# Attention's value product: the last key tile as doubled half tiles, the odd key apart, keys dealt to groups by 400

## The chip, the cores and the metric

The kernel runs on one core of a Trainium2 chip. The metric is the device time of one execution in microseconds (us); lower is better. A core has five engines with queues of their own: TensorE (PE in the profile; its weight loads are PEld), VectorE (DVE), ScalarE (ACT), GpSimd (POOL) and SyncE (SP), which here only issues the DMA transfers. They meet through semaphores.

## The reference, cut to what matters

Cross attention of 64 queries for each of 32 batches over 1601 context rows, 16 heads, then a recurrent mixing layer and a two-layer feed-forward, each with a residual. The change touches the attention alone:

```python
q = query @ w_q
k, v = jnp.split(context @ w_kv, 2, axis=-1)
scores = jnp.einsum('bhqd,bhkd->bhqk', q, k) * SCALE
attn = jax.nn.softmax(scores, axis=-1)
out = jnp.einsum('bhqk,bhkd->bhqd', attn, v)
```

The kernel multiplies the queries by the key weights first (`write_queries`), so that the scores are a product with the raw context (192 columns), and it multiplies the softmax with the raw context too; the value weights come in a later stage (`attention_output`). A product in full fp32 accuracy is made of fp32r products: a tensor x is split in x_hi (rounded) and x_lo = x - x_hi.

## The kernel before

`attend_batches` runs 32 batches of 8 steps, 256 steps in all; a step is 128 query rows (of the 16 x 64) against all 1601 keys. The loop holds two batches (16 steps) a pass. In step s the engines do this, each in its own order:

- TensorE: 20 matmuls of the scores of step s, in four chunks of 288, 512, 512 and 290 keys, then the product of step s-4 (`product`, LAG = 4): 13 key tiles of 128 keys, each with two matmuls, `pt_hi` against 384 columns (the context's high and low part side by side, `nat`), and `pt_lo` against 192 columns (the high part). The product of one step starts as its first low half (`pt_lo_done`) is there, and needs the second from the seventh tile on.
- VectorE: row maxima of the left and of the right half of the scores (L714, L716), their combination (L719), the output of the product of step s-5 (`out`, L695 and L701), then, when both exponentials are done, a transpose of the whole probability row in 32x32 blocks (L725, 1664 columns with 63 of padding) into `turned`, the sum of the row (L726) and its reciprocal (L728).
- ScalarE: `high` (L614) rounds the landed, transposed probabilities of step s-4 to `pt_hi` in two halves of 6 and 7 tiles, `half_out` (L605) scales half of the accumulator, a piece of the next batch is rounded in some steps, then come the two exponentials of step s (L646). There is one `pt_hi`, so `high` waits for the product before to end (`acc_ready`), and for the transfers of its pair of steps (`moved`).
- GpSimd: `low` (L550), the two halves of `pt_lo`, and one piece of the next batch in most steps.
- SyncE issues every transfer of the stage, in program order. `move(m)` (L485) carries two steps' blocks from `turned` to `landed` in 16 transfers, since a block of keys has to change its partitions. `load_raw(n + 1)` (L452) fetches the next batch's context rows. A batch n of the queue is: `load_ct_a`, `move(4n-1)`, `load_qk`, `store`, `load_qk`, `move(4n)`, `load_raw`, `load_ct_b` (L464, L465), `move(4n+1)`, `load_ct_b`, `store`, `move(4n+2)`, `load_ct_a`. `move(m)` waits until the transposes of steps 2m and 2m+1 are done.

Keys sit in four groups of 32 partitions. Before, group g takes 416 keys in a row (13 tiles of 32), and the last group gets the 353 that are left and zeros. So the context rows of a batch come in five transfers:

```python
    for g in reversed(range(GROUPS)):
        tiles, at = (TILES if g < GROUPS - 1 else whole), g * TILES * ROWS
        rows = src[at:at + tiles * ROWS, :].rearrange("(t x) c -> x t c", x=ROWS)
        yield raw[g * ROWS:(g + 1) * ROWS, 0:tiles, :], rows
```

Of the kernel before, what the change touches and what calls it, by code (L numbers as in the profile page):

```python
# [37 lines left out]

GROUPS, ROWS = 4, 32
TILES = -(-NKV // P)  # L40
PADDED = GROUPS * TILES * ROWS
HALVES = [(0, 802), (802, NKV + NKV % 2)]
# [48 lines left out]
def write_queries(nc, x, w_q, wkT, qk_dram, ctx_in, ctxT_in, shared, turned):  # L91
# [7 lines left out]
    with ExitStack() as ctx:  # L99
# [30 lines left out]
        padded, raw_free, first_in = sem("padded"), sem("raw_free"), sem("first_in")  # L130
        first_a, first_q, first_b = first_views(turned)
# [7 lines left out]
        def _(sp):  # L139
# [21 lines left out]
            sp.wait_ge(raw_free, 1)  # L161
# [11 lines left out]
            sp.wait_ge(first_in, 16 * (3 + GROUPS + 1 + 3))  # L173

        @block.gpsimd
        def _(pool):
            identity(nc, pool, ident, ident_done)
            nc.gpsimd.memset(turned[:, :, NKV:NKV + 1], 0.0).then_inc(padded, 1)

            pool.wait_ge(wq_hi_done, 1)  # L180
            nc.gpsimd.tensor_tensor(wq_lo[:, :, :], wq[:, :, :], bits(wq_hi[:, :, :]), ALU.subtract).then_inc(wq_lo_done, 1)
            pool.wait_ge(wk_hi_done, 1)
            nc.gpsimd.tensor_tensor(wks_lo[:, :, :], wks[:, :, :], bits(wks_hi[:, :, :]), ALU.subtract).then_inc(wk_lo_done, 1)
            pool.wait_ge(wk_lo_done, 1)
            pool.wait_ge(tp_ready, NT)
            nc.gpsimd.memset(raw[(GROUPS - 1) * ROWS:P, :, :], 0.0).then_inc(raw_free, 1)
# [184 lines left out]
def attend_batches(nc, ctx_in, ctxT_in, qk_dram, o_dram, shared, turned):  # L371
# [15 lines left out]
    CW = NKV + NKV % 2  # L387
# [7 lines left out]
    with ExitStack() as ctx:  # L395
# [14 lines left out]
        part, o_q = sb("part", [P, DC]), sb("o_q", [P, DC])  # L410
        o_t = shared[:, KT * DC:KT * DC + DC * SB].rearrange("p (k s x) -> p k s x", s=SB, x=R)
# [20 lines left out]
        acc_ready, part_done, acc_read, o_done = sem("acc_ready"), sem("part_done"), sem("acc_read"), sem("o_done")  # L432
# [3 lines left out]
        first_a, first_q, first_b = first_views(turned)  # L436
# [12 lines left out]
        def _(sp):  # L449
# [46 lines left out]
            def body(r, first, last):  # L496
                for u in range(SPB):
# [32 lines left out]
            sp.wait_ge(padded, 2)  # L530
# [10 lines left out]
        def _(pool):  # L541

            nc.gpsimd.memset(stage[:, 1, NKV - CHALF[1][0]:CW - CHALF[1][0]], 0.0).then_inc(padded, 1)
            nc.gpsimd.memset(prob[:, NKV:PW], 0.0).then_inc(padded, 1)
# [52 lines left out]
        def _(act):  # L597
            def half_out(p, ring, par, fresh):

                act.wait_ge(acc_ready, p + 1)  # L600
                act.wait_ge(rinv_done, p + 1)
                if not fresh:

                    act.wait_ge(acc_read, p)
                nc.scalar.activation(part[:, :], acc[par][:, DC:2 * DC], ACT.Copy, scale=rinv[:, ring:ring + 1]).then_inc(part_done, 1)  # L605

            def high(p, count, slot, fresh):

                act.wait_ge(moved[slot // 2], count)
                if not fresh:  # L610

                    act.wait_ge(acc_ready, p)
                for t0, t1 in THALF:
                    nc.scalar.activation(pt_hi[:, t0:t1, :, :], by_tile(slot, t0, t1), ACT.Copy).then_inc(pt_hi_done, 1)  # L614
# [15 lines left out]
            def prepare_nat(n, h, par, fresh):  # L630

                t0, t1 = THALF[h]
                act.wait_ge(raw_in, n * 80)
                if not fresh:

                    act.wait_ge(acc_ready, n * SB - SB)
                nc.scalar.activation(nat[par][:, t0:t1, 0:DC], raw[:, t0:t1, :], ACT.Copy).then_inc(nat_hi_done, 1)

            def step(r, j, first):
                s, par = r * SPP + j, j % 2  # L640
                act.wait_ge(max_done, s + 1)
                if not (first and j == 0):

                    act.wait_ge(turned_done, s)
                for h, (lo, hi, done) in enumerate(((0, MID, exp_left), (MID, NKV, exp_done))):
                    nc.scalar.activation(prob[:, lo:hi], scores[:, S0 + lo:S0 + hi], ACT.Exp, bias=negmax[:, par:par + 1],  # L646
                                         accum_out=rowsum[:, par, h:h + 1]).then_inc(done, 1)

            def drain(r, j, first):
                if not (first and j < LAG + 1):  # L650
                    half_out(r * SPP + (j - LAG - 1), (j - LAG - 1) % SB, (j - LAG - 1) % 2, first and j == LAG + 1)
# [20 lines left out]
            for h, (lo, hi) in enumerate(CHALF):  # L672
# [15 lines left out]
        def _(dve):  # L688
            def out(p, ring, par, fresh_half, first):

                dve.wait_ge(part_done, p + 1)
# [19 lines left out]
            def step(r, j, first):  # L711
# [16 lines left out]
                nc.vector.reciprocal(rinv[:, j % SB:j % SB + 1], rowtot[:, par:par + 1]).then_inc(rinv_done, 1)  # L728

# [4 lines left out]

            lower = slice(DCB, P)
# [20 lines left out]
        def _(pe):  # L756
# [21 lines left out]
            def product(r, j, first):  # L778
# [5 lines left out]
                for h, (t0, t1) in enumerate(THALF):  # L784
# [803 lines left out]
```

## Time and profile before

| | |
|---|---|
| median of 3 runs | 2571.8 us (2565.84 to 2573.11) |
| the profiled execution: time | 2574.86 us |
| its span, first to last instruction | 2573.1 us |
| attention's steady stretch (200 to 2067 us) | 1867 us, TensorE busy 1862 us of it |
| granted TensorE clock, whole span | 0.958 |

The profile is of one execution. Busy time counts an engine's instructions; matmuls are pipelined, so a matmul's duration is longer than the distance from its start to the start of the next. "Landing" is the time from the issue of a transfer until its semaphore is raised. SPq is SP's queue: there an instruction's duration is the time in which it is being issued. What is rated is the difference to the runs' median.

### The profile page before, as it was taken

The numbers are of one execution on the slowest core, as the hardware profiler recorded it, in microseconds if no ns is written. First come the engines' busy times: TensorE is split into PE (matmuls) and PEld (weight loads), VectorE is DVE, ScalarE is ACT, GpSimd is POOL, SyncE is SP. The second block draws the span as 40 slices with busy tenths as digits, with TensorE's granted clock in tenths as the row PEclk, the third lists the DMA queues.
The fourth block names the chain that finished last, engine by engine and source line by source line (L and its number), as shares of the span: only waits on it lengthen the run. The fifth ranks groups of instructions, "written<-read, shape, count | busy, mean of one in ns | idle before, by whom it ended". The sixth has DMA issues, their size and how long they took to land. (4 is left out here: it accounts for less than half of the span.)

```text
span 2573.1 us, 43052 instructions
## 1 busy us (share of the span) xinstructions
PE 2355.1 (92%) x13872; PEld 2145.3 (83%) x13872; DVE 1710.9 (66%) x2666; ACT 1516.0 (59%) x2459; POOL 1700.7 (66%) x873
## 2 busy tenths in 40 slices
PE   4969999999999999999999999999999947855777
PEld 3649999999999999999999999999999945744666
DVE  7766666666666666666666666666666626768762
ACT  4646666666666666666666666666666525543342
POOL 2007788888888888888888888888888632023452
PEclk9989999999999999999999999999999968986888
DMA  5957878888788888888777788878888549910000
GB/s 158 259 155 190 193 193 198 194 192 193 194 192 195 199 194 195 197 198 197 192 193 195 192 193 200 196 192 199 196 198 195 131 102 219 187 50 0 9 9 17
DMA packets 387378, 434.18 MB, mean 169 GB/s; under 512 B 45652, under 2 KB 362232, under 8 KB 387320
## 3 DMA queue, kind: packets, MB, share of 16 engines
q1 hardware_dynamic: 387320, 433.45, 69.2%
q8 instruction: 32, 0.52, 0.1%
q14 instruction: 26, 0.21, 0.0%
HBM read 162.73 MB, written 52.43 MB: 84 GB/s over the span
## 5 line engine op out<-in xcount | busy, mean ns | idle before, releaser
L550 POOL TENSOR_TENSOR p_pt_lo<-p_landed,p_pt_hi 128x768 fp32r<-128x768 f32 (+1 forms) x512 | 1005.1, 1985 | 359.9 <-ACT p_pt_hi L614 359.9
L789 PE MATMUL p_acc<-p_nat,p_pt_hi 128*128 128x384 f32 x3328 | 978.5, 362 | 14.1 <-POOL p_pt_lo L550 13.8
L791 PE MATMUL p_acc<-p_nat,p_pt_lo 128*128 128x192 f32 x3328 | 845.7, 254 | 0.0
L646 ACT ACTIVATE p_prob<-p_scores,p_negmax 128x800 f32<-128x800 f32 (+1 forms) x512 | 471.2, 926 | 515.7 <-DVE p_negmax L719 515.7
L773 PE MATMUL p_scores<-p_ct_hi,p_q_hi 128*128 128x512 f32 (+2 forms) x2048 | 710.2, 350 | 24.2 <-DVE p_ct_hi L746 13.8
L773 PE MATMUL p_scores<-p_ct_hi,p_q_lo 128*128 128x512 f32 (+2 forms) x2048 | 705.1, 348 | 0.0
L725 DVE STREAM_TRANSPOSE turned<-p_prob 128x1664 f32<-128x1664 f32 x256 | 489.5, 1912 | 317.0 <-ACT p_prob L646 317.0
L789 PEld LDWEIGHTS p_acc<-p_nat,p_pt_hi 128*128 128x128 f32 x3328 | 630.7, 190 | 16.5 <-issue 13.7
L791 PEld LDWEIGHTS p_acc<-p_nat,p_pt_lo 128*128 128x128 f32 x3328 | 640.8, 193 | 0.0
L614 ACT ACTIVATE p_pt_hi<-p_landed 128x768 fp32r<-128x768 f32 (+1 forms) x512 | 432.3, 892 | 159.2 <-PE p_acc L791 152.5
L773 PEld LDWEIGHTS p_scores<-p_ct_hi,p_q_hi 128*128 128x128 f32 x2048 | 388.8, 190 | 71.9 <-issue 14.3
L773 PEld LDWEIGHTS p_scores<-p_ct_hi,p_q_lo 128*128 128x128 f32 x2048 | 390.7, 191 | 44.7
L716 DVE TENSOR_REDUCE p_halfmax<-p_scores 128x1 f32<-128x801 f32 x256 | 254.1, 993 | 212.7 <-PE p_scores L773 212.7
L773 PE MATMUL p_scores<-p_ct_lo,p_q_hi 128*128 128x512 f32 (+2 forms) x1024 | 354.2, 346 | 0.0
L714 DVE TENSOR_REDUCE p_halfmax<-p_scores 128x1 f32<-128x800 f32 x256 | 253.7, 991 | 59.5 <-PE p_scores L773 52.3
L773 PEld LDWEIGHTS p_scores<-p_ct_lo,p_q_hi 128*128 128x128 f32 x1024 | 194.3, 190 | 22.3
L577 POOL TENSOR_TENSOR p_nat<-shared,p_nat 128x1152 fp32r<-128x1152 f32 (+1 forms) x62 | 178.5, 2879 | 0.0
L562 POOL TENSOR_TENSOR p_q_lo<-p_stage,p_q_hi 128x1024 fp32r<-128x1024 f32 x62 | 148.5, 2395 | 15.2 <-ACT p_q_hi L624 15.2
L695 DVE SCALAR_TENSOR_TENSOR p_o_q<-p_acc,p_rinv,p_part 128x192 f32<-128x192 f32 x256 | 107.0, 418 | 35.3 <-ACT p_part L605 34.4
L605 ACT ACTIVATE p_part<-p_acc,p_rinv 128x192 f32<-128x192 f32 x256 | 103.0, 402 | 31.4 <-PE p_acc L791 31.4
L558 POOL TENSOR_TENSOR p_ct_lo<-p_stage,p_ct_hi 128x802 fp32r<-128x802 f32 (+1 forms) x62 | 109.5, 1767 | 14.2 <-ACT p_ct_hi L621 14.2
L569 POOL TENSOR_TENSOR p_ct_hi<-p_stage,p_ct_hi 64x802 fp32r<-64x802 f32 (+1 forms) x62 | 109.0, 1757 | 5.6 <-POOL p_pt_lo L550 0.5
(190 smaller groups left out, 2652.9 us busy)
## 6 DMA issues: line engine op xcount, KB each, us to landing
p_landed<-turned SPq DMA_DIRECT2D x2048, 104.0 KB, 2.2
shared<-in_ctx SPq DMA_DIRECT2D x96, 312.0 KB
o_scratch<-shared SPq DMA_DIRECT2D x256, 96.0 KB, 2.6
qk_scratch<-p_out_a SPq DMA_DIRECT2D x16, 1024.0 KB, 4.6
p_oa<-o_scratch SPq DMA_DIRECT2D x32, 512.0 KB, 6.0
p_stage<-qk_scratch SPq DMA_DIRECT2D x31, 512.0 KB, 3.9
p_stage<-qk_scratch SPq DMA_DIRECT2D x62, 256.0 KB, 4.2
p_stage<-in_ctxT SPq DMA_DIRECT2D x31, 401.0 KB, 3.2
```

What stands on the lines that cost most here:

```text
L550: nc.gpsimd.tensor_tensor(pt_lo[:, t0:t1, :, :], by_tile(slot, t0, t1), bits(pt_hi[:, t0:t1, :, :]), ALU.subtract).then_inc(pt_lo_done, 1)
L558: nc.gpsimd.tensor_tensor(ct_lo[1 - par][:, lo:hi], stage[:, u, 0:hi - lo], bits(ct_hi[1 - par][:, 0, lo:hi]), ALU.subtract).then_inc(ct_a ...
L562: nc.gpsimd.tensor_tensor(stepped(q_lo[1 - par][:, u - 3, :]), by_step(stage[:, u - 3, :]), bits(stepped(q_hi[1 - par][:, u - 3, :])), ALU ...
L577: nc.gpsimd.tensor_tensor(x[:, t0:t1, DC:2 * DC], raw[:, t0:t1, :], bits(x[:, t0:t1, 0:DC]), ALU.subtract).then_inc(nat_done, 1)
L614: nc.scalar.activation(pt_hi[:, t0:t1, :, :], by_tile(slot, t0, t1), ACT.Copy).then_inc(pt_hi_done, 1)
L646: nc.scalar.activation(prob[:, lo:hi], scores[:, S0 + lo:S0 + hi], ACT.Exp, bias=negmax[:, par:par + 1], accum_out=rowsum[:, par, h:h + 1] ...
L714: nc.vector.tensor_reduce(halfmax[:, par, 0:1], scores[:, S0:S0 + MID], AX.X, ALU.max, negate=True).then_inc(halfmax_done, 1)
L716: nc.vector.tensor_reduce(halfmax[:, par, 1:2], scores[:, S0 + MID:S0 + NKV], AX.X, ALU.max, negate=True).then_inc(halfmax_done, 1)
L725: nc.vector.transpose(turned[:, j % 4, :], prob[:, :]).then_inc(turned_done, 1)
L773: last = nc.tensor.matmul(scores[:, S0 + lo:S0 + hi], w, x, start=m == 0, stop=m == len(terms) - 1)
L789: nc.tensor.matmul(acc[k % 2][:, 0:2 * DC], pt_hi[:, t, :, :].rearrange("p i x -> p (i x)"), x[:, t, :], start=t == 0, stop=False, skip_gr ...
L791: last = nc.tensor.matmul(acc[k % 2][:, 0:DC], pt_lo[:, t, :, :].rearrange("p i x -> p (i x)"), x[:, t, 0:DC], start=False, stop=t == KT - ...
```

## The change

Group g now takes 400 keys in a row, 12 whole tiles of 32 and 16 more. The 1600 keys so make 12 whole tiles of 128, and a thirteenth that holds 64 keys twice: in each group's 32 partitions 16 keys, and the same 16 again. `pt_hi` of this tile is `landed` times a column `second` that is 0 in the first sixteen and 1 in the second sixteen partitions of each group; `pt_lo` = landed - `pt_hi` is then the whole probability in the first and the low part in the second. One matmul of `pt_lo` against 384 columns does the tile, where two stood. Key 1601, the odd one, is left out of the product: VectorE keeps its probability and multiplies it by the reciprocal of the row sum, ScalarE scales the key's context row with it (a row held on all partitions, one more transfer a batch), and VectorE adds both halves of the accumulator to this in two instructions.

```diff
 def raw_pieces(raw, ctx_in, n):
     src = ctx_in[bass.ds(n, 1), :, :].rearrange("a k c -> (a k) c")
-    whole = (NKV - (GROUPS - 1) * TILES * ROWS) // ROWS
     for g in reversed(range(GROUPS)):
-        tiles, at = (TILES if g < GROUPS - 1 else whole), g * TILES * ROWS
-        rows = src[at:at + tiles * ROWS, :].rearrange("(t x) c -> x t c", x=ROWS)
-        yield raw[g * ROWS:(g + 1) * ROWS, 0:tiles, :], rows
-    tail = (GROUPS - 1) * TILES * ROWS + whole * ROWS
-    yield raw[(GROUPS - 1) * ROWS:(GROUPS - 1) * ROWS + NKV - tail, whole, :], src[tail:NKV, :]
+        at = g * SPAN
+        yield raw[g * ROWS:(g + 1) * ROWS, 0:FULL, :], src[at:at + FULL * ROWS, :].rearrange("(t x) c -> x t c", x=ROWS)
+        for h in range(2):
+            yield raw[g * ROWS + h * REST:g * ROWS + (h + 1) * REST, FULL, :], src[at + FULL * ROWS:at + SPAN, :]
+def odd_key(ctx_in, n):
+    return ctx_in[bass.ds(n, 1), NKV - 1:NKV, :].rearrange("a k c -> (a k c)").partition_broadcast(P)
...
# SyncE, after move(4n+2)
+                    if not ends:
+                        if not begins:
+                            sp.wait_ge(share_done, n * SB)
+                        sp.dma_start(odd_row[:, 1 - u, :], odd_key(ctx_in, n + 1)).then_inc(odd_in, 16)
...
# ScalarE
-                act.wait_ge(acc_ready, p + 1)
-                act.wait_ge(rinv_done, p + 1)
-                nc.scalar.activation(part[:, :], acc[par][:, DC:2 * DC], ACT.Copy, scale=rinv[:, ring:ring + 1]).then_inc(part_done, 1)
+                act.wait_ge(odd_done, p + 1)
+                nc.scalar.activation(part[:, :], odd_row[:, batch_par, :], ACT.Copy, scale=odd_share[:, ring:ring + 1]).then_inc(share_done, 1)
...
                 for t0, t1 in THALF:
-                    nc.scalar.activation(pt_hi[:, t0:t1, :, :], by_tile(slot, t0, t1), ACT.Copy).then_inc(pt_hi_done, 1)
+                    last = t1 == KT
+                    done = nc.scalar.activation(pt_hi[:, t0:t1 - last, :, :], by_tile(slot, t0, t1 - last), ACT.Copy)
+                    if last:
+                        done = nc.scalar.activation(pt_hi[:, KT - 1:KT, :, :], by_tile(slot, KT - 1, KT), ACT.Copy, scale=second[:, 0:1])
+                    done.then_inc(pt_hi_done, 1)
...
# VectorE
                 nc.vector.scalar_tensor_tensor(o_q[:, :], acc[par][:, 0:DC], rinv[:, ring:ring + 1], part[:, :], ALU.mult,
+                                               ALU.add).then_inc(summed_done, 1)
+                dve.wait_ge(summed_done, p + 1)
+                nc.vector.scalar_tensor_tensor(o_q[:, :], acc[par][:, DC:2 * DC], rinv[:, ring:ring + 1], o_q[:, :], ALU.mult,
                                                ALU.add).then_inc(acc_read, 1)
...
-                nc.vector.transpose(turned[:, j % 4, :], prob[:, :]).then_inc(turned_done, 1)
+                nc.vector.tensor_copy(odd_p[:, j % SB:j % SB + 1], prob[:, NKV - 1:NKV]).then_inc(odd_kept, 1)
+                by_group = prob[:, 0:NKV - 1].rearrange("p (g k) -> p g k", g=G)
+                slot = turned[:, j % 4, :].rearrange("p (g k) -> p g k", g=G)
+                nc.vector.transpose(slot[:, :, 0:FULL * R], by_group[:, :, 0:FULL * R])
+                rest = by_group[:, :, FULL * R:SPAN].unsqueeze(2).broadcast_to([P, G, 2, REST])
+                nc.vector.transpose(slot[:, :, FULL * R:GK].rearrange("p g (h x) -> p g h x", h=2), rest).then_inc(turned_done, 1)
...
+                nc.vector.tensor_tensor(odd_share[:, j % SB:j % SB + 1], odd_p[:, j % SB:j % SB + 1], rinv[:, j % SB:j % SB + 1],
+                                        ALU.mult).then_inc(odd_done, 1)
...
# TensorE
-                    for t in range(t0, t1):
+                    for t in range(t0, min(t1, KT - 1)):
                         nc.tensor.matmul(acc[k % 2][:, 0:2 * DC], pt_hi[:, t, :, :].rearrange("p i x -> p (i x)"), x[:, t, :], start=t == 0, stop=False,
...
+                last = nc.tensor.matmul(acc[k % 2][:, 0:2 * DC], pt_lo[:, KT - 1, :, :].rearrange("p i x -> p (i x)"), x[:, KT - 1, :], start=False,
+                                        stop=True, skip_group_check=True)
```

What stands in the rows of the engines moves at two places. The first is SP's queue in the loop, between `move(4n)`, whose 16 transfers are the row ahead, and `load_ct_b`, whose first is the row behind. ISA and REGISTER_ALU rows are address arithmetic. Before:

```order
L452 ISA
L452 DMA shared<-in_ctx 32x11x192
L452 ISA
L452 DMA shared<-in_ctx 32x13x192
L452 ISA
L452 DMA shared<-in_ctx 32x13x192
L452 REGISTER_ALU
L452 DMA shared<-in_ctx 32x13x192
L452 ISA
L452 DMA shared<-in_ctx 1x192
L464 ISA
```

And of the changed kernel, the first two and a half of the four groups, which all have this pattern:

```order
L460 ISA
L460 DMA shared<-in_ctx 32x12x192
L460 ISA
L460 DMA shared<-in_ctx 16x192 x2
L460 ISA
L460 DMA shared<-in_ctx 32x12x192
L460 ISA
L460 DMA shared<-in_ctx 16x192 x2
L460 ISA
L460 DMA shared<-in_ctx 32x12x192
```

Five transfers have become twelve, four of 32 partitions and eight of 16, and they stay ahead of `move(4n+1)` in the queue.

The second place is the end of a step on VectorE, from the step's output to the next step's first maximum. Before:

```order
L695 SCALAR_TENSOR_TENSOR p_o_q<-p_acc,p_rinv,p_part 128x192
L701 STREAM_TRANSPOSE shared<-p_o_q 128x6x32
L724 ISA
L725 STREAM_TRANSPOSE turned<-p_prob 128x1664
L726 TENSOR_REDUCE p_rowtot<-p_rowsum 128x1
L728 RECIPROCAL p_rinv<-p_rowtot 128x1
L713 REGISTER_ALU
L714 TENSOR_REDUCE p_halfmax<-p_scores 128x1
```

And in the changed kernel:

```order
L726 SCALAR_TENSOR_TENSOR p_o_q<-p_acc,p_rinv,p_part 128x192
L729 SCALAR_TENSOR_TENSOR p_o_q<-p_acc,p_rinv,p_o_q 128x192
L735 STREAM_TRANSPOSE shared<-p_o_q 128x6x32
L758 ISA
L759 COPY p_odd_p<-p_prob 128x1
L762 STREAM_TRANSPOSE turned<-p_prob 128x4x384
L764 STREAM_TRANSPOSE turned<-p_prob 128x4x32
L765 TENSOR_REDUCE p_rowtot<-p_rowsum 128x1
L767 RECIPROCAL p_rinv<-p_rowtot 128x1
L770 TENSOR_TENSOR p_odd_share<-p_odd_p,p_rinv 128x1
L747 REGISTER_ALU
L748 TENSOR_REDUCE p_halfmax<-p_scores 128x1
```

A second addition stands ahead of the transpose, a copy and a second transpose between the exponentials and `turned_done`, and a multiplication of two columns between the reciprocal and the next maximum.

## Rows read from the trace of the kernel before

**Rows 1.** Part 1 of the page: engine, busy us (share of span) xinstructions.

```profile
PE 2355.1 (92%) x13872; PEld 2145.3 (83%) x13872; DVE 1710.9 (66%) x2666; ACT 1516.0 (59%) x2459; POOL 1700.7 (66%) x873
```

**Rows 2.** Windows, steady stretch: length, each engine's busy us, TensorE clock, DMA.

```profile
200.20:2067.00 1866.80, 1862.33 (x11588) 1750.69 (x11587) 1257.34 (x2016) 1209.23 (x2008) 1522.08 (x751) 1.00 0.80 192
```

**Rows 3.** Waits, 1100 to 1974 us: total us, times, longest us.

```profile
DVE p_halfmax L716 <- PE p_scores L773: 99.1, 119, 0.9
ACT p_pt_hi L614 <- PE p_acc L791: 71.6, 118, 0.6
```

**Rows 4.** Timeline of SP's queue, part of a batch: start us, us, instruction.

```profile
1015.67 10.37 SPq L485 DMA_DIRECT2D p_landed<-turned  x16
1026.23 2.46 SPq L452 DMA_DIRECT2D shared<-in_ctx  x5
1028.90 0.54 SPq L464 DMA_DIRECT2D p_stage<-in_ctxT  x1
1029.55 0.53 SPq L465 DMA_DIRECT2D p_stage<-in_ctxT  x1
1030.40 10.41 SPq L485 DMA_DIRECT2D p_landed<-turned  x16
```

**Rows 5.** Waits of SP's queue, 1100 to 1974 us, columns as in Rows 3.

```profile
SPq L480 <- DVE turned L725: 25.8, 29, 1.2
SPq L458 <- POOL p_ct_hi L569: 22.4, 15, 1.7
```

**Rows 6.** By source line, 600 to 1200 us: issue ns min/median/max.

```profile
L452 SPq DMA_DIRECT2D shared<-in_ctx x50: 243/346/458, 612.6 to 1146.7; - x50
...
L485 SPq DMA_DIRECT2D p_landed<-turned x651: 587/602/677, 602.0 to 1199.4; - x163
```

**Rows 7.** DMA, 1040.1 to 1041 us: issues, KB each, us to landing.

```profile
p_landed<-turned SPq DMA_DIRECT2D x2, 104.0 KB, 2.4
```

**Rows 8.** Timeline of DVE, big transposes: start us, us, [idle before <-releaser].

```profile
1013.62 1.91 DVE L725 STREAM_TRANSPOSE turned<-p_prob 128x1664 f32<-128x1664 f32 x1 [1.04 <-ACT p_prob L646]
...
1028.38 1.91 DVE L725 STREAM_TRANSPOSE turned<-p_prob 128x1664 f32<-128x1664 f32 x1 [1.15 <-ACT p_prob L646]
...
1072.70 1.92 DVE L725 STREAM_TRANSPOSE turned<-p_prob 128x1664 f32<-128x1664 f32 x1 [1.24 <-ACT p_prob L646]
```

**Rows 9.** Timeline after that transfer: ACT, POOL and PE, one product.

```profile
1043.73 1.69 ACT L614 ACTIVATE p_pt_hi<-p_landed 128x768 fp32r<-128x768 f32 x2 [0.62 <-PE p_acc L791]
...
1041.16 2.66 POOL L577 TENSOR_TENSOR p_nat<-shared,p_nat 128x1152 fp32r<-128x1152 f32 x1
1044.65 3.93 POOL L550 TENSOR_TENSOR p_pt_lo<-p_landed,p_pt_hi 128x768 fp32r<-128x768 f32 x2 [0.82 <-ACT p_pt_hi L614]
...
1047.14 0.34 PE L789 MATMUL p_acc<-p_nat,p_pt_hi 128*128 128x384 f32 x1
1047.32 0.25 PE L791 MATMUL p_acc<-p_nat,p_pt_lo 128*128 128x192 f32 x1
1047.41 0.36 PE L789 MATMUL p_acc<-p_nat,p_pt_hi 128*128 128x384 f32 x1
...
1048.84 0.36 PE L789 MATMUL p_acc<-p_nat,p_pt_hi 128*128 128x384 f32 x1
```

**Rows 10.** Groups by form, 600 to 1200 us: count, busy us, mean ns.

```profile
L701 DVE STREAM_TRANSPOSE shared<-p_o_q 128x192 f32<-128x192 f32 x81 | 30.7, 379 | 4.3
...
L719 DVE TENSOR_REDUCE p_negmax<-p_halfmax 128x1 f32<-128x2 f32 x81 | 12.6, 155 | 2.8
```

**Rows 11.** Timeline in the last stage: POOL and DVE at once.

```profile
2306.25 6.28 POOL L1183 TENSOR_TENSOR p_w_lo<-p_area,p_w_hi 128x2048 fp32r<-128x2048 f32 x1 [1.81 <-ACT p_w_hi L1297]
...
2309.45 3.10 DVE L1316 TENSOR_TENSOR p_parts<-p_stats 128x4 f32<-128x4 f32 x1
```

**Rows 12.** Windows, end of the attention stage, columns as in Rows 2.

```profile
2063.00:2067.00 4.00, 0.77 (x6) 0.80 (x6) 2.34 (x5) 1.99 (x3) 2.73 (x2) 1.00 0.23 55
2067.20:2070.40 3.20, 3.20 (x15) 3.20 (x13) 0.00 (x0) 0.00 (x0) 0.94 (x1) 0.50 0.69 164
```

More of the change, by code:

```diff
@@ L39 @@
 GROUPS, ROWS = 4, 32
-TILES = -(-NKV // P)
+TILES = -(-(NKV - 1) // P)
 PADDED = GROUPS * TILES * ROWS
+SPAN = (NKV - 1) // GROUPS
+FULL = SPAN // ROWS
+REST = SPAN - FULL * ROWS
+assert NKV - 1 == GROUPS * SPAN and TILES == FULL + 1 and 2 * REST == ROWS
+PIECES = 3 * GROUPS
 HALVES = [(0, 802), (802, NKV + NKV % 2)]
@@ L410, in attend_batches @@
         part, o_q = sb("part", [P, DC]), sb("o_q", [P, DC])
+        odd_row, odd_p, odd_share = sb("odd_row", [P, 2, DC]), sb("odd_p", [P, SB]), sb("odd_share", [P, SB])
+        second, second_of = sb("second", [P, 1]), sb("second_of", [P, G])
         o_t = shared[:, KT * DC:KT * DC + DC * SB].rearrange("p (k s x) -> p k s x", s=SB, x=R)
@@ L543, in _ @@
             nc.gpsimd.memset(stage[:, 1, NKV - CHALF[1][0]:CW - CHALF[1][0]], 0.0).then_inc(padded, 1)
-            nc.gpsimd.memset(prob[:, NKV:PW], 0.0).then_inc(padded, 1)
+            nc.gpsimd.memset(second_of[:, :], 1.0).then_inc(second_done, 1)
+            pool.wait_ge(second_done, 1)
+            nc.gpsimd.affine_select(out=second_of[:, :], in_=second_of[:, :], compare_op=ALU.is_ge, fill=0.0, base=-REST,
+                                    pattern=[[-R, G]], channel_multiplier=1).then_inc(second_done, 1)
+            pool.wait_ge(second_done, 2)
+            nc.gpsimd.affine_select(out=second_of[:, :], in_=second_of[:, :], compare_op=ALU.is_ge, fill=0.0, base=R - 1,
+                                    pattern=[[R, G]], channel_multiplier=-1).then_inc(second_done, 1)
             def low(p, slot):
@@ L597, in _, with share @@
         def _(act):
-            def half_out(p, ring, par, fresh):
-                act.wait_ge(acc_ready, p + 1)
-                act.wait_ge(rinv_done, p + 1)
+            def share(p, ring, batch_par, loaded, fresh):
+                act.wait_ge(odd_done, p + 1)
+                if fresh:
+                    act.wait_ge(odd_copied, 1)
+                elif loaded is not None:
+                    act.wait_ge(odd_in, loaded)
                 if not fresh:
-                    act.wait_ge(acc_read, p)
-                nc.scalar.activation(part[:, :], acc[par][:, DC:2 * DC], ACT.Copy, scale=rinv[:, ring:ring + 1]).then_inc(part_done, 1)
+                    act.wait_ge(summed_done, p)
+                nc.scalar.activation(part[:, :], odd_row[:, batch_par, :], ACT.Copy, scale=odd_share[:, ring:ring + 1]).then_inc(share_done, 1)
             def high(p, count, slot, fresh):
@@ L650, in drain @@
                 if not (first and j < LAG + 1):
-                    half_out(r * SPP + (j - LAG - 1), (j - LAG - 1) % SB, (j - LAG - 1) % 2, first and j == LAG + 1)
+                    k = j - LAG - 1
+                    loaded = (r * SPB + k // SB) * 16 if k % SB == 0 else None
+                    share(r * SPP + k, k % SB, k // SB % 2, loaded, first and k == 0)
             def raise_high(r, j, first):
@@ L732, in body @@
                     step(r, j, first)
+            dve.wait_ge(second_done, 3)
+            nc.vector.tensor_reduce(second[:, :], second_of[:, :], AX.X, ALU.max).then_inc(second_done, 1)
             lower = slice(DCB, P)
@@ L787, in product @@
                     pe.wait_ge(pt_lo_done, p * 2 + (h + 1))
-                    for t in range(t0, t1):
+                    for t in range(t0, min(t1, KT - 1)):
                         nc.tensor.matmul(acc[k % 2][:, 0:2 * DC], pt_hi[:, t, :, :].rearrange("p i x -> p (i x)"), x[:, t, :], start=t == 0, stop=False,
                                          skip_group_check=True)
-                        last = nc.tensor.matmul(acc[k % 2][:, 0:DC], pt_lo[:, t, :, :].rearrange("p i x -> p (i x)"), x[:, t, 0:DC], start=False,
-                                                stop=t == KT - 1, skip_group_check=True)
+                        nc.tensor.matmul(acc[k % 2][:, 0:DC], pt_lo[:, t, :, :].rearrange("p i x -> p (i x)"), x[:, t, 0:DC], start=False,
+                                         stop=False, skip_group_check=True)
+                last = nc.tensor.matmul(acc[k % 2][:, 0:2 * DC], pt_lo[:, KT - 1, :, :].rearrange("p i x -> p (i x)"), x[:, KT - 1, :], start=False,
+                                        stop=True, skip_group_check=True)
                 last.then_inc(acc_ready, 1)
```

39 lines of the change are left out of this document (21 added, 18 removed).

## The prediction

> **What bounds the kernel now.** I read the engines' shares first, then the windows, then the waits, and last the queue of SP. TensorE is busy 92% of the span [rows 1]; in the attention's steady stretch it is busy 1862 of 1867 us, at a granted clock of 1.00, its upper level of 2.4 GHz [rows 2]. No wait of TensorE stands among the waits there. The others wait for it: VectorE's second maximum waits 0.83 us a step for the scores (99.1 us in 119), `high` 0.61 us for the product before to end [rows 3]. So TensorE's issue rate sets the step, 59.08 us a batch: two transposes one batch apart end at 1015.53 and 1074.62 [rows 8].
>
> The reader should then look at what is nearly as long. SP's queue issues without a break: 16 transfers of `move(4n)` in 10.37 us, the five of `load_raw`, two of `load_ct_b`, and 16 of `move(4n+1)` in 10.41 us [rows 4]. Over 15 batches it waits 25.8 us for transposes and 22.4 us for a piece of GpSimd's [rows 5], 3.2 us a batch. It is busy 55.9 of 59.1 us with nothing but issuing. And it stands in a ring. A transpose ends at 1015.53 [rows 8], `move(4n)` starts at 1015.67, `load_raw` at 1026.23, `load_ct_b` at 1028.90, and `move(4n+1)` starts at 1030.40 [rows 4], just after its own transpose ends at 1030.29 [rows 8]; SP itself was free at 1030.08, so there are 0.2 us of slack. Its last transfer is issued at about 1040.2 and lands 2.4 us later [rows 7], at 1042.6. `high` starts at 1043.73, released by TensorE: 1.1 us of slack. GpSimd has the second low half at 1048.58, and TensorE, which began this product at 1047.14, needs it at 1048.84, with its seventh tile [rows 9]: 0.3 us of slack. From there it is TensorE's work to the scores after the next two products, and from them to the transpose at 1072.70. Without the slack of 1.6 us the ring is **57.5 us** long, against 59.1 that TensorE takes. That is all the room SP has.
>
> **TensorE's gain.** One matmul of 192 columns goes in each of 256 products. Its recorded 0.25 us isn't what it costs: the next matmul starts 0.09 us after it, while a whole tile takes 0.27 to 0.29 us [rows 9]. I take 0.10 us, so 0.8 us a batch and 26 us in all: TensorE's work is 58.3 us a batch.
>
> **SP's queue, which this gain runs into.** `load_raw` takes 2.67 us now, to the start of `load_ct_b` [rows 4], 0.53 us a transfer: 0.35 for the transfer [rows 6], 0.19 for its registers. After, four large transfers at 0.53 are 2.1 us. Eight small ones need registers once 0.19 and once 0.11 us a pair (the latter is 1028.90 to 1029.55 less 0.54 [rows 4]), 1.2 us together, and eight times their own duration. No row shows 16 partitions by one row. The bounds: 0.24 us, the minimum of `load_raw`, its piece of one row; 0.60 us, the median of `move`'s [rows 6]; between them lie 0.35 us, and 0.54 us of `load_ct_b` with one row for each of 64 partitions [rows 4]. By shape it is between the one row and the 64, so I take 0.40: 2.1 + 1.2 + 3.2 = 6.5 us, **3.9 us more than now**. At 0.24 it is 2.6 more, at 0.60 it is 5.5.
>
> What is queued behind is `move(4n+1)`, which carries two steps' probabilities. It starts late, lands late, and `high` of step 8n+2, `low` and the product wait in turn. The odd row's transfer costs some 0.55 us of SP (0.35 and 0.19), but lies where SP waits 1.5 us a batch for GpSimd [rows 5]: nothing, and if that cover were gone it would be part of SP's sum only, 55.9 + 3.9 + 0.6 = 60.4 us a batch, less than the ring below.
>
> The Trainium skill ("DMA: Bandwidth & Descriptors", section "Issuing engines are not separate DMA queues") says that the time to initiate DMAs "is usually small relative to the DMA itself". By it the seven added transfers would cost nothing and the first rival below would hold. This trace has 0.60 us of issue for 2.4 us to landing, sixteen in a row, in a queue that is busy 95% of the time.
>
> **VectorE.** In the ring: a copy of one column (0.16 us, as L719 [rows 10]) and the fixed part of a second transpose. 1664 columns take 1.91 us [rows 8], 192 take 0.38 [rows 10]: 1.04 ns a column and 0.18 fixed. Together 0.35 us before `turned_done`. Outside: the multiplication, 0.2 us, hidden with these in the 0.83 us of slack [rows 3]. The second addition (0.4 us, about a 192-column pass [rows 10]) lies in the 1.0 to 1.2 us that VectorE waits for the exponentials ahead of the transpose [rows 8].
>
> The multiplication reads two columns that both lie in SBUF, at a time when GpSimd mostly computes. That can cost time: an addition of 4 columns on VectorE took 3.10 us and ended at 2312.55, GpSimd's at 2312.53 [rows 11]. Here `low` starts at 1044.65 [rows 9], four steps or 29.5 us earlier at 1015.1, and its first half, of 3.93 us in two, ends at 1017.1. The transpose ends at 1015.53 [rows 8]; with 0.35 us more and some 0.4 for the row sum and the reciprocal the multiplication stands ready at 1016.3 and is held 0.7 us. That and its own 0.2 are about the 0.83 us of slack [rows 3], and TensorE waits for no exponential today. I charge nothing. The skill ("SBUF — State Buffer", section "SBUF: two separate sides") has the rule: VectorE with two SBUF inputs and a GpSimd operation that reads SBUF lock each other out for a whole instruction; by it the hold-up is this 0.7 us, and the trace agrees.
>
> **ScalarE.** One activation of 128 columns more a step, below 0.4 us. It comes ahead of GpSimd's second half, which starts 1.95 us after its first; the two of `high` take 1.69 us [rows 9] and start 0.9 us earlier. Hidden. `half_out` keeps its length and no longer waits for the product. At the start, column `second` puts three small GpSimd operations ahead of VectorE's first work: +1 us once.
>
> **The sum.** Ring: 57.5 + 3.9 (SP) + 0.35 (VectorE) - 0.3 (three shortened products in it) = 61.4 us, over TensorE's 58.3. So TensorE stands still 3.1 us a batch, in one piece, ahead of a product. After a gap of that size the clock falls: near the attention's end TensorE works 0.77 of 4.0 us, and the next 3.2 us are granted 0.50, the 1.2 GHz level [rows 12]. That stretch gives back half of its 3.4 us: +1.7 us, and it is in the ring. Per batch 61.4 - 59.1 + 1.7 = 4.0 us; `load_raw` runs 31 times: +124. With the 1 us at the start the profiled execution's 2574.9 (2573.1 of span and 1.8 around it) becomes 2700. It lies 3 us above the median of the runs, so for a median **2697 us**, 4.9% slower.
>
> Ends of this case: 0.24 us a transfer and no fall of the clock, 57.5 + 2.6 + 0.05 = 60.15, +1.1 a batch, 2606. At 0.60 and with the fall 63.05 + 1.7, +5.6 a batch, 2747. Without the fall at 0.40 it is 2645.
>
> **Rivals.**
> - *The issue is hidden, TensorE's gain stays.* For it: the DMA engines are busy 0.80 only [rows 2], and the transfers are tiny. Against: SP's own time counts, not theirs. It decides where the ring falls to 58.3, that is with under 0.8 us more than now, twelve transfers in 3.4 us, 0.29 us each with registers; every transfer seen takes 0.24 without them. Then 2572 - 26 + 1 = 2547 us. Chance 0.07; half-way, within 0.3% of before, another 0.05.
> - *VectorE becomes the bound.* Its own loop is 7.39 - 0.83 = 6.55 us a step now. Add 0.35 and 0.2, and let GpSimd hold both the multiplication (0.35 on average) and the copy (in the four steps a batch in which it runs a long piece until after the exponentials end, as 1041.16 + 2.66 = 1043.82 [rows 9], some 0.7 us): 8.15 us in four steps a batch, 0.8 over 7.39, 3.1 a batch, 2572 + 96 = 2668 us. Against: one column has no second input. Chance 0.10.
> - *SP's ring*, as above: 0.78. The clock falls in three quarters of it.
>
> **The numbers.** A difference of 0.3% (8 us) is about what a measurement of this kernel can tell from none. Faster 0.07, same 0.05, slower 0.88. The range takes the ring's ends and VectorE's case with it, 2600 to 2755; outside are the first rival and a clock that falls for longer.
>
> **What the profile after would show.** TensorE idle some 96 us before the product's first matmuls (L834), in about 31 gaps of 3 us, one a batch; `high` (L638) waiting for a DMA about 31 times; SP's small transfers (L460) at 0.40 us; the clock at about 0.97 in the steady stretch; VectorE's big transposes together at 2.1 us. The prediction is wrong if the small transfers issue in under 0.1 us, if `high` still waits for TensorE alone, or if the steps are all alike and long (then it is VectorE).

## The result and the profile after

The changed kernel takes **2650.15 us** in the median of four runs (2647.23 to 2651.82), where the kernel before takes 2572.45 (2565.84 to 2576.3) beside it: 1.0304 times, with a 95% interval of 1.028 to 1.0327. That is slower, 77.7 us against the 125 predicted, and inside the range. The profiled execution's span is 2645.5 us.

The page of the changed kernel, its shares and some of its costliest groups, which answer to [rows 1] and to the lines of the kernel before:

```profile
PE 2354.4 (89%) x13616; PEld 2134.1 (81%) x13616; DVE 2013.4 (76%) x3691; ACT 1572.4 (59%) x2716; POOL 1700.1 (64%) x874
...
PEclk9989999999999999999999999999999987986888
...
L834 PE MATMUL p_acc<-p_nat,p_pt_hi 128*128 128x384 f32 x3072 | 928.8, 367 | 85.4 <-POOL p_pt_lo L568 83.1
...
L638 ACT ACTIVATE p_pt_hi<-p_landed 128x768 fp32r<-128x768 f32 x512 | 404.8, 838 | 317.4 <-PE p_acc L838 200.2
```

TensorE fell from 92% to 89% of the span. In the attention its idle time stands ahead of matmuls of the product (L834): 85.4 us, of which 83.1 were ended by the low half. The clock line is a 9 nearly throughout, so the clock isn't the main part.

The windows of the changed kernel: the steady stretch as in [rows 2], a batch in which the clock fell, a batch in which it didn't, and around the gap of each the 4 us before and the 3.2 us after:

```profile
core 0: us, PE busy (x) PEld busy (x) DVE busy (x) ACT busy (x) POOL busy (x), PEclk, DMA share, GB/s
200.20:2120.00 1919.80, 1846.33 (x11200) 1725.81 (x11199) 1532.25 (x2980) 1250.48 (x2234) 1507.98 (x742) 0.99 0.75 188
1144.00:1206.20 62.20, 60.06 (x361) 56.33 (x360) 49.44 (x96) 40.29 (x73) 48.77 (x24) 0.97 0.74 187
1206.20:1267.20 61.00, 58.72 (x360) 54.79 (x360) 49.28 (x96) 40.50 (x73) 48.83 (x24) 1.00 0.78 192
1142.10:1146.10 4.00, 1.93 (x11) 1.49 (x9) 2.80 (x6) 2.74 (x5) 1.81 (x2) 1.00 0.81 213
1146.20:1149.40 3.20, 3.20 (x12) 3.20 (x13) 1.93 (x4) 1.95 (x5) 3.12 (x2) 0.50 0.62 150
1204.30:1208.30 4.00, 1.88 (x11) 1.42 (x9) 2.76 (x6) 2.72 (x5) 1.80 (x2) 1.00 0.81 207
1208.40:1211.60 3.20, 3.09 (x20) 2.85 (x21) 1.93 (x4) 1.97 (x5) 3.12 (x2) 1.00 0.65 160
```

By the starts of `load_raw`, a batch is 61.0 us long with the clock at its upper level of 2.4 GHz, and 62.2 us where 3.2 us of it were granted 0.50, the 1.2 GHz level. The mean from one batch to the next, past the first batches, is 61.5 us against 59.1 before: 2.4 us a batch, 75 in 31 batches, which is nearly all of the 77.7. TensorE did less before the gap that left the clock alone (1.88 of 4.0 us) than before the one after which it fell (1.93). Of the 26 gaps from 468 us on, all of 2.04 to 2.33 us, 10 were followed by such a fall, each with 1.2 us. In the whole attention stand 13 falls: two early ones, at 341 and 406 us, are 6.8 us long and lie in batches of 65.2 and 63.9 us, and the last comes at its end, at 2071 us.

Where the 2 us arise. SP's queue in the changed kernel, from one transpose pair's `move` to the next (start, duration, line):

```profile
1236.49 10.32 SPq L493 DMA_DIRECT2D p_landed<-turned  x16
1246.99 5.87 SPq L460 DMA_DIRECT2D shared<-in_ctx  x12
1253.05 0.55 SPq L472 DMA_DIRECT2D p_stage<-in_ctxT  x1
1253.70 0.54 SPq L473 DMA_DIRECT2D p_stage<-in_ctxT  x1
1254.47 7.78 SPq L493 DMA_DIRECT2D p_landed<-turned  x12
```

And who waited at the far end of it, in the timeline of all engines at that place (start, duration; in brackets the idle time ahead and what ended it):

```profile
1266.49 1.58 ACT L638 ACTIVATE p_pt_hi<-p_landed 128x768 fp32r<-128x768 f32 x2 [3.35 <-DMA p_landed<-turned]
...
1266.94 0.29 PE L818 MATMUL p_scores<-p_ct_hi,p_q_lo 128*128 128x290 f32 x1
...
1267.41 3.89 POOL L568 TENSOR_TENSOR p_pt_lo<-p_landed,p_pt_hi 128x768 fp32r<-128x768 f32 x2 [3.52 <-ACT p_pt_hi L638]
...
1269.27 0.44 PE L834 MATMUL p_acc<-p_nat,p_pt_hi 128*128 128x384 f32 x1 [2.04 <-POOL p_pt_lo L568]
```

From the start of `load_raw` to that of `load_ct_b` it is 6.06 us; [rows 4] had 2.67. Before, SP waited another 0.2 us there for a transpose, which it no longer does; so the second `move` (L493) starts 18.0 us behind the first, where it was 14.7. In the second view the reader follows it to the end: `high` sits idle for 3.35 us until a transfer has landed, `low` for 3.52 us until `high`, and TensorE, whose last scores' matmul began at 1266.94, stands still for 2.04 us until `low`.

That isn't all that TensorE waits. Its timeline from the end of this gap to the seventh tile, and below it the same after a gap behind which the clock fell:

```profile
1270.79 0.36 PE L834 MATMUL p_acc<-p_nat,p_pt_hi 128*128 128x384 f32 x1
1270.99 0.25 PE L836 MATMUL p_acc<-p_nat,p_pt_lo 128*128 128x192 f32 x1
1271.35 0.44 PE L834 MATMUL p_acc<-p_nat,p_pt_hi 128*128 128x384 f32 x1
...
1146.15 0.67 PE L834 MATMUL p_acc<-p_nat,p_pt_hi 128*128 128x384 f32 x1 [2.12 <-POOL p_pt_lo L568]
...
1149.29 0.36 PE L836 MATMUL p_acc<-p_nat,p_pt_lo 128*128 128x192 f32 x1
1149.45 0.45 PE L834 MATMUL p_acc<-p_nat,p_pt_hi 128*128 128x384 f32 x1
```

The seventh tile follows the matmul ahead of it by 0.36 us (1270.99 to 1271.35), where 0.09 is usual: TensorE has caught up with `low` and waits another 0.27 us for its second half, which ends at 1271.30. With the 2.2 us ahead of the product and a slower first tile behind each of the two stops, that makes the 2.7 us by which 61.0 us is longer than TensorE's 58.3. From the first to the seventh tile it is 2.08 us here and 3.30 us where the clock fell: 1.2 us more. Six tiles took 1.5 us longer, and 0.27 of that TensorE would have waited anyway. It is so behind all ten steady falls (3.15 to 3.31 us) and behind the 16 other gaps (2.06 to 2.09 us).

One line's own answers for the small and large transfers of `load_raw` (minimum, median, maximum in ns), and for VectorE's two new instructions:

```profile
L460 SPq DMA_DIRECT2D shared<-in_ctx x372: 317/362/1832, 194.8 to 2052.2; - x186
...
L770 DVE TENSOR_TENSOR p_odd_share<-p_odd_p,p_rinv x256: 159/932/1361, 177.0 to 2142.9; 128x1 f32<-128x1 f32 x128
...
L759 DVE COPY p_odd_p<-p_prob x256: 153/154/156, 174.7 to 2140.6; 128x1 f32<-128x1 f32 x128
```

The multiplication of one column takes 0.16 us at best, 0.93 in the median and, by the page, 0.745 on average; the copy takes 0.15 in each of 256 steps. VectorE's timeline of the changed kernel in a step in which the multiplication is long:

```profile
1219.50 0.15 DVE L759 COPY p_odd_p<-p_prob 128x1 f32<-128x1 f32 x1 [0.76 <-ACT p_prob L674]
1219.57 1.77 DVE L762 STREAM_TRANSPOSE turned<-p_prob 128x1536 f32<-128x1536 f32 x1
1221.26 0.27 DVE L764 STREAM_TRANSPOSE turned<-p_prob 128x128 f32<-128x128 f32 x1
...
1221.81 1.00 DVE L770 TENSOR_TENSOR p_odd_share<-p_odd_p,p_rinv 128x1 f32<-128x1 f32 x1
```

GpSimd's timeline in the same step, up to the end of its first half:

```profile
1220.93 1.86 POOL L568 TENSOR_TENSOR p_pt_lo<-p_landed,p_pt_hi 128x768 fp32r<-128x768 f32 x1 [1.37 <-ACT p_pt_hi L638]
```

The first of GpSimd's two halves ends at 1222.79, and the multiplication at 1222.81. It is so throughout: 190 of the 256 multiplications took longer than 0.3 us, each of them began while an instruction of GpSimd ran, and each ended 0.01 to 0.02 us behind that instruction's end.

### The profile page after: what moved, and what is told of

The parts are those of the page before. It is cut to its first block and busy times, and to the rows that moved or that the text cites. A ratio compares the mean times of both kernels' runs of the same rounds, so it can differ in the third digit from the quotient of the medians.

```text
span 2645.5 us, 44700 instructions
## 1 busy us (share of the span) xinstructions
PE 2354.4 (89%) x13616; PEld 2134.1 (81%) x13616; DVE 2013.4 (76%) x3691; ACT 1572.4 (59%) x2716; POOL 1700.1 (64%) x874
## 5 line engine op out<-in xcount | busy, mean ns | idle before, releaser
L834 PE MATMUL p_acc<-p_nat,p_pt_hi 128*128 128x384 f32 x3072 | 928.8, 367 | 85.4 <-POOL p_pt_lo L568 83.1
L836 PE MATMUL p_acc<-p_nat,p_pt_lo 128*128 128x192 f32 x3072 | 786.5, 256 | 0.0
L834 PEld LDWEIGHTS p_acc<-p_nat,p_pt_hi 128*128 128x128 f32 x3072 | 592.2, 193 | 99.3 <-POOL p_pt_lo L568 77.7
L836 PEld LDWEIGHTS p_acc<-p_nat,p_pt_lo 128*128 128x128 f32 x3072 | 601.6, 196 | 0.0
L638 ACT ACTIVATE p_pt_hi<-p_landed 128x768 fp32r<-128x768 f32 x512 | 404.8, 838 | 317.4 <-PE p_acc L838 200.2
L762 DVE STREAM_TRANSPOSE turned<-p_prob 128x1536 f32<-128x1536 f32 x256 | 452.7, 1768 | 0.0
L759 DVE COPY p_odd_p<-p_prob 128x1 f32<-128x1 f32 x256 | 39.5, 154 | 210.4 <-ACT p_prob L674 210.4
L770 DVE TENSOR_TENSOR p_odd_share<-p_odd_p,p_rinv 128x1 f32<-128x1 f32 x256 | 190.8, 745 | 8.7
L726 DVE SCALAR_TENSOR_TENSOR p_o_q<-p_acc,p_rinv,p_part 128x192 f32<-128x192 f32 x256 | 107.0, 418 | 46.7 <-PE p_acc L838 25.4
```

Of the source, the lines that this page charges most:

```text
L638: done = nc.scalar.activation(pt_hi[:, t0:t1 - last, :, :], by_tile(slot, t0, t1 - last), ACT.Copy)
L762: nc.vector.transpose(slot[:, :, 0:FULL * R], by_group[:, :, 0:FULL * R])
L770: nc.vector.tensor_tensor(odd_share[:, j % SB:j % SB + 1], odd_p[:, j % SB:j % SB + 1], rinv[:, j % SB:j % SB + 1], ALU.mult).then_inc(odd ...
```

## The experiments

Experiments 1 to 4 ran beside the kernel before at 2571.76 us (2568.0 to 2577.67), 5 to 7 beside it at 2572.01 (2569.95 to 2575.57).

**1. The kernel before, with twelve transfers in `load_raw`.** Keys, TensorE, VectorE and ScalarE work as before; the groups' last 32 rows are fetched apart, in halves of 16 for three of the four.

```diff
-        rows = src[at:at + tiles * ROWS, :].rearrange("(t x) c -> x t c", x=ROWS)
-        yield raw[g * ROWS:(g + 1) * ROWS, 0:tiles, :], rows
+        rows = src[at:at + (tiles - 1) * ROWS, :].rearrange("(t x) c -> x t c", x=ROWS)
+        yield raw[g * ROWS:(g + 1) * ROWS, 0:tiles - 1, :], rows
+        half = ROWS // 2 if g < GROUPS - 1 else ROWS
+        for h in range(ROWS // half):
+            first = at + (tiles - 1) * ROWS + h * half
+            yield raw[g * ROWS + h * half:g * ROWS + (h + 1) * half, tiles - 1, :], src[first:first + half, :]
```

> The kernel before with its context rows fetched in twelve transfers a batch instead of five (six of them of 16 partitions), and nothing else of the change. Theory (SP's ring): the slot between move(4n) and move(4n+1) grows by some 3.3 us, the ring from 57.5 to 60.8 us a batch against 59.1 now, +53 us, and up to 15 more where the clock falls: 2625 to 2642 us. TensorE waits about 2 us a batch ahead of one product. Rival (VectorE's additions make the loss, issuing is hidden): no difference to before, 2572 us.

Measured: 2645.62 us (2644.59 to 2648.81), 1.0281 times before (1.026 to 1.0302). Seven more transfers alone make nearly the whole loss, 73.9 us of 77.7. The time is 3.6 us above the upper end of what I expected. SP's queue in this run, at the same place of the loop, and one batch later:

```profile
1246.50 5.91 SPq L456 DMA_DIRECT2D shared<-in_ctx  x12
1252.60 0.55 SPq L468 DMA_DIRECT2D p_stage<-in_ctxT  x1
...
1254.03 10.38 SPq L489 DMA_DIRECT2D p_landed<-turned  x16
...
1307.58 6.12 SPq L456 DMA_DIRECT2D shared<-in_ctx  x12
1313.88 0.55 SPq L468 DMA_DIRECT2D p_stage<-in_ctxT  x1
```

The windows of this run for one batch:

```profile
1206.20:1267.50 61.30, 59.68 (x369) 55.67 (x368) 39.79 (x64) 38.66 (x65) 48.88 (x25) 1.00 0.76 189
```

TensorE's timeline where the gap of that batch ends:

```profile
1268.86 0.44 PE L793 MATMUL p_acc<-p_nat,p_pt_hi 128*128 128x384 f32 x1 [1.37 <-POOL p_pt_lo L554]
```

The slot is 6.10 us, 3.4 more than before, as after, and 6.30 in the next batch; so it goes on in turn, and the batches take 61.0 and 61.3 us in turn. The ring of 57.5 us with 3.4 more is 60.9; the mean batch has 61.2. So my ring was 0.3 us too short. TensorE's gap is shorter than in the changed kernel, since TensorE has 0.8 us more to do a batch. From 472 us on there are 26 gaps of 1.34 to 1.57 us, and the clock fell after none; ahead of them it fell after three of four gaps of 2.24 to 2.81 us.

**2. The change without its eight small transfers.** They are left out from the second batch on, so that the thirteenth key tile holds another batch's rows.

```diff
-                for dst, src in raw_pieces(raw, ctx_in, n):
-                    sp.dma_start(dst, src).then_inc(raw_in, 16)
+                for i, (dst, src) in enumerate(raw_pieces(raw, ctx_in, n)):
+                    if i % 3 == 0:
+                        sp.dma_start(dst, src).then_inc(raw_in, 16)
```

> The changed kernel without the eight small transfers in the loop (the last key tile's context rows stay those of batch 0, so this tile's part of the product is wrong from batch 1 on); VectorE, ScalarE and TensorE do all of the change. Theory (SP's ring): the slot is 0.5 us shorter than before, no stall, TensorE's 58.3 us a batch bound again: 2547 us, 2541 to 2556. Rival (VectorE's additions or the held multiplication are the bound): above 2620 us.

Measured: 2552.3 us (2551.81 to 2552.87), 0.9919 times before (0.9899 to 0.994). All that the change adds to VectorE and ScalarE is in it, held multiplication included, and it is faster than before. Against it, the eight small transfers cost 98 us in the changed kernel (2650.15 less 2552.3). Its windows for one batch:

```profile
1145.10:1203.40 58.30, 58.30 (x363) 54.81 (x362) 50.66 (x97) 40.61 (x73) 48.85 (x25) 1.00 0.83 199
```

Its waits from 1100 to 1974 us, those of `high`:

```profile
ACT p_pt_hi L639 <- PE p_acc L839: 58.6, 115, 0.5
ACT p_pt_hi L639 <- DMA p_landed<-turned: 5.0, 5, 2.3
```

TensorE is busy for all of 58.30 us, just what the prediction gave it as its own work, and `high` waits for TensorE again.

**3. The small transfers at another place of SP's queue**, behind `move(4n+2)` and the odd row; ScalarE waits for them ahead of its second piece of the context (`tail_in`).

```diff
-                        load_raw(n + 1)
+                        load_raw(n + 1, False)
...
                         sp.dma_start(odd_row[:, 1 - u, :], odd_key(ctx_in, n + 1)).then_inc(odd_in, 16)
+                        load_raw(n + 1, True)
```

> The changed kernel with the eight small transfers moved in SP's queue to behind move(4n+2), beside the odd row's, where SP used to wait; as many transfers as in the changed kernel. Theory (a ring through one slot, not the count of transfers): the first slot is free again; the second grows from 4.2 us to some 5.8, its ring reaches 59.2 us, and SP's whole sum of 59.9 us a batch bounds: 2597 us, 2575 to 2615. Rival (what counts is only how many transfers SP issues, or the DMA engines' load): as the changed kernel, 2650 us.

Measured: 2597.16 us (2591.88 to 2601.55), 1.01 times before (1.0073 to 1.0127). The change is 25 us slower than before here, and 78 with the transfers in their first place; against experiment 2, the same transfers cost 45 us here and 98 there. The waits of SP's queue from 1100 to 1974 us, all that there are:

```profile
SPq L494 <- POOL p_pt_lo L570: 9.3, 16, 0.6
```

The waits of `high` in the same stretch:

```profile
ACT p_pt_hi L640 <- DMA p_landed<-turned: 46.3, 44, 1.7
...
ACT p_pt_hi L640 <- PE p_acc L842: 32.6, 59, 1.5
```

SP waits for 9.3 us in nearly 15 batches, 0.6 a batch, and otherwise issues; `high` waits for transfers three times a batch, a little each. So SP is busy in all but 0.6 us of the mean batch's 59.8, and I read its sum as the bound: 55.9 us before, 3.4 for the small transfers and 0.57 for the odd row (0.38 to issue, 0.19 for its registers) are 59.9. That the sum meets the batch so closely is partly luck, since SP was busy for 59.2 of it. No experiment shortens SP's sum alone here, so this bound is read from the waits and not shown.

**4. The multiplication in another form**, by a scalar operand, so that one tensor is read.

```diff
-                nc.vector.tensor_tensor(odd_share[:, j % SB:j % SB + 1], odd_p[:, j % SB:j % SB + 1], rinv[:, j % SB:j % SB + 1],
-                                        ALU.mult).then_inc(odd_done, 1)
+                nc.vector.tensor_scalar(odd_share[:, j % SB:j % SB + 1], odd_p[:, j % SB:j % SB + 1], rinv[:, j % SB:j % SB + 1],
+                                        None, ALU.mult).then_inc(odd_done, 1)
```

> The changed kernel with the multiplication of the odd key's probability by the reciprocal written as a tensor by a scalar column, which has one tensor input, so that GpSimd should not hold it (0.16 us in place of 0.75 on average). Theory (SP's ring): VectorE's wait is beside the ring, so at most 0.2 us a batch comes back: 2642 to 2652 us. Rival (VectorE is the bound through this hold-up): most of the loss comes back, 2550 to 2590 us.

Measured: 2650.86 us (2647.76 to 2661.4), 1.0317 times before (1.0287 to 1.0347). The line of the multiplication:

```profile
L770 DVE TENSOR_SCALAR p_odd_share<-p_odd_p,p_rinv x256: 212/214/216, 177.4 to 2142.9; 128x1 f32<-128x1 f32 x128
```

0.21 us in all 256 steps, where it was 0.745 on average: the edit took away 0.5 us a step, 4.3 a batch, and the time stays. VectorE isn't on the path.

**5. The small transfers on ScalarE's queue**, two in each of the last four steps of a batch, ahead of the step's exponentials; all of the computation is done.

```diff
-                for dst, src in raw_pieces(raw, ctx_in, n):
-                    sp.dma_start(dst, src).then_inc(raw_in, 16)
+                for i, (dst, src) in enumerate(raw_pieces(raw, ctx_in, n)):
+                    if i % 3 == 0:
+                        sp.dma_start(dst, src).then_inc(raw_in, 16)
...
+                    if u >= 4 and not ends:
+                        small = [piece for i, piece in enumerate(raw_pieces(raw, ctx_in, n + 1)) if i % 3]
+                        act.wait_ge(nat_done, n * 2 + 2)
+                        for dst, src in small[2 * u - 8:2 * u - 6]:
+                            act.dma_start(dst, src).then_inc(tail_in, 16)
```

> The changed kernel with the eight small transfers issued from ScalarE's queue, two in each of the steps 4 to 7 of a batch, where ScalarE waits some 2 us for the row maximum. Everything of the change is computed. Theory (SP's ring): as without these transfers, TensorE's 58.3 us a batch bound: 2547 us, 2541 to 2560 (ScalarE's issuing may cost a little in step 5). Rival (DMA engines or VectorE bound): above 2620 us.

Measured: 2556.06 us (2552.37 to 2558.53), 0.9937 times before (0.9919 to 0.9955): faster than both kernels, if by 0.6% only, with the whole change in it, and 4 us above experiment 2. The line of the transfers on ScalarE's queue:

```profile
L706 ACTq DMA_DIRECT2D shared<-in_ctx x248: 317/382/645, 197.5 to 1982.9; - x124
```

The windows of this kernel from 200.2 to 2030 us:

```profile
200.20:2030.00 1829.80, 1825.90 (x11222) 1708.22 (x11221) 1582.68 (x2992) 1256.89 (x2238) 1512.43 (x745) 1.00 0.82 197
```

They are no shorter to issue there (0.38 us), but ScalarE has the room, and TensorE is busy again in all but 3.9 of 1829.8 us.

**6. Both of the last two edits.**

> The run before this one (small transfers on ScalarE's queue) and the multiplication with one tensor input as well. Theory: VectorE's hold-up is beside the path also when TensorE bounds, so no more than 5 us below the run with the transfers alone: 2540 to 2555 us. Rival (the hold-up begins to count once SP's stall is gone): 10 to 30 us below that run.

Measured: 2553.83 us (2550.78 to 2559.24), 0.9927 times before (0.9905 to 0.9949). Beside 0.9937 (0.9919 to 0.9955) that tells no difference: the held multiplication costs nothing that can be seen even where TensorE is the bound.

**7. TensorE's gain alone**: the kernel before without the last tile's matmul of 192 columns. The low part of the last tile's probabilities is left out.

```diff
-                        nc.tensor.matmul(acc[k % 2][:, 0:2 * DC], pt_hi[:, t, :, :].rearrange("p i x -> p (i x)"), x[:, t, :], start=t == 0, stop=False,
-                                         skip_group_check=True)
-                        last = nc.tensor.matmul(acc[k % 2][:, 0:DC], pt_lo[:, t, :, :].rearrange("p i x -> p (i x)"), x[:, t, 0:DC], start=False,
...
+                        last = nc.tensor.matmul(acc[k % 2][:, 0:2 * DC], pt_hi[:, t, :, :].rearrange("p i x -> p (i x)"), x[:, t, :], start=t == 0,
...
+                        if t < KT - 1:
+                            nc.tensor.matmul(acc[k % 2][:, 0:DC], pt_lo[:, t, :, :].rearrange("p i x -> p (i x)"), x[:, t, 0:DC], start=False,
+                                             stop=False, skip_group_check=True)
```

> The kernel before with the last key tile's 192-column matmul left out and nothing else (so that tile's low part is missing from the output): the gain of the change by itself. Theory: 0.10 us a product, 26 us: 2546 us, 2541 to 2551. Rival (the recorded 0.25 us is what a matmul costs): 2508 us. Second rival (SP's ring of 57.5 us plus jitter bounds first): 2555 us or more.

Measured: 2546.57 us (2546.16 to 2548.24), 0.9901 times before (0.9885 to 0.9918). 25.4 us by 256 products are 0.10 us a matmul, and its mean batch is 58.31 us.

## Why the prediction was right, and what was mis-sized

- **What bounds: right.** TensorE sets the step, and SP's ring lies a little below, 1.6 us as predicted, 1.3 as measured. Experiments 2 and 7 put TensorE's work at 58.3 us a batch, the number of the prediction. The ring is 0.3 us longer than it was read from single rows: experiment 1, which adds nothing else, has 61.2 and not 60.9. Most of it lies on SP's queue: from the start of `load_raw` to the second `move` it is 7.5 and 7.7 us in turn in experiment 1, where the 4.0 of [rows 4] without its slack and 3.4 make 7.4. The other pieces of the ring are within 0.2 us of what was read, and TensorE waits at the seventh tile, where the prediction had its last slack.
- **TensorE's gain: right**, 0.10 us a matmul (experiment 7), in place of the recorded 0.25.
- **SP's queue: right in kind, 0.5 us too large.** 3.4 us more and not 3.9: a small transfer takes 0.36 us and not 0.40, which is 0.3, and 0.1 is rounding, since the prediction's 6.5 less 2.67 is 3.8. Of all loss, 73.9 us come with these transfers alone (1), and nothing of it is left without them (2) or with them on another queue (5).
- **VectorE in the ring: 0.2 us too large.** From the copy's start to the second transpose's end it is 2.03 us (1219.50 to 1221.53), where one transpose took 1.91 [rows 8]: 0.12 more and not 0.35, because the three overlap by some 0.08 us each.
- **The held multiplication: right**, and in the place that was named. It was to be held 0.7 us and to end with the first of GpSimd's halves; its median is 0.93 us against 0.16 free, and it ends 0.02 us behind that half. That it costs nothing is shown by experiments 4 and 6. The rule of the Trainium skill ("SBUF — State Buffer", section "SBUF: two separate sides"), which the prediction drew on, agrees with three rows: with two inputs in SBUF 0.93 us, the copy with one input 0.154 and at most 0.156, though GpSimd was at work at its start in 157 of the 256 steps, and the product with a scalar operand 0.21 in every step.
- **ScalarE: right.** The activation it gained takes 0.39 us and is hidden: from the start of `high` to the end of `low` it is 4.8 us in the changed kernel as in the one before.
- **The odd row's transfer: right** that it is hidden in the changed kernel's order; in experiment 3, where I read SP's sum as the bound, it is a term of it.
- **The clock: the step that was mis-sized most.** "That stretch gives back half of its 3.4 us: +1.7 us", in every batch, was 53 of the 124 us. TensorE stands still for 2.7 us a batch and not 3.1, and not in one piece: 2.2 us ahead of the product, the rest at the seventh tile and in the restarts. The clock fell in 10 of the 26 steady batches. A fall costs 1.2 us, since it slows only the six tiles up to the wait for the second low half, and takes up that wait. These falls gave back 12 us, and the two long ones early in the attention some 5 more. Experiment 1 shows that with gaps of 1.5 us the clock falls in none of the steady batches.

The terms as measured: 57.8 (ring) + 3.4 + 0.12 - 0.3 = 61.0 us, the batch without a fall; with 0.5 us a batch for the falls 61.5, 2.4 more than before; 31 batches are 75 us, and 77.7 were measured. The prediction's 4.0 a batch are too large by 1.2 of the clock, 0.5 of SP and 0.2 of VectorE, and too small by the ring's 0.3. Its case without a fall (2645) was by chance nearest: there two terms too large by 0.7 us a batch stood for the falls that did occur and the ring's 0.3.

Of the signs that it named, `high` waits for a transfer once a batch (14 times from 1100 to 1974 us), and TensorE's idle time ahead of L834 is 85 us for 96; the clock of the steady stretch is 0.99 and not 0.97.

**The rivals.** The hidden issue (2547 us) is refuted by experiment 1; its time is nearly what experiments 2 and 5 reach (2552 and 2556) once SP has nothing more to do. By the rule of the Trainium skill that the time to initiate DMAs "is usually small relative to the DMA itself" ("DMA: Bandwidth & Descriptors", section "Issuing engines are not separate DMA queues") the kernel would have been faster; here twelve transfers took 5.87 us of a queue. VectorE as the bound (2668 us) is refuted by experiment 2, which has all of VectorE's additions and no loss, by the copy, held in no step, and by experiment 4.

Open: what decides after which of the gaps of 2.04 to 2.33 us the clock falls (their length doesn't: it fell after one of 2.08 and not after one of 2.30), and whether SP's sum is the bound in experiment 3. No run here tests these.

## What to carry to other kernels

When a change adds small transfers, look at the issuing queue as at an engine: sum what it issues in a period, and find the ring in which it stands, before looking at bytes or DMA engines. Where the queue's ring has some 1.5 us to spare, eight small transfers cost 98 us (3.8%) in one place of the order, 45 (1.8%) in another, and 4 on another engine's queue, each against the same kernel without them (experiment 2). Take a loss that depends on the clock falling as one end of a range, not as a term for every period.

## What was unexpected of the hardware

- A transfer of 16 rows takes 0.36 us to issue (0.33 in experiment 1), one of 64 rows by one row 0.55 (1253.05), and 32 partitions by 12 rows 0.33 to 0.45. The number of bytes doesn't set it.
- The clock fell after 10 of 26 gaps of nearly one length, and after none of 26 gaps of 1.34 to 1.57 us.
- Behind such a fall a key tile of the product took 0.53 us (1146.15 to 1149.45 is six of them and a restart) where it takes 0.29, and the stretch of 3.4 us at the lower level cost 1.2 us, because part of it fell into a wait.
- A product of two columns on VectorE took 0.16 us free and 0.93 in the median; when it was held, it ended within 0.02 us behind GpSimd's instruction. With a scalar operand it took 0.21, never more than 0.216.
